# One stage for the seam between two layers of a graph network: gates, gated sum, second norm, layer-1 node products and the placing of logits in five groups of tiles

## The reference, cut to what matters

```python
xn = _layernorm(x)
x = x + gnn0(xn) + mix0(xn)
x = x + ffn0(_layernorm(x))            # four experts, mixed by gates
xn = _layernorm(x)                     # the "second norm"
x = x + gnn1(xn) + mix1(xn)            # mix1 ends in _layernorm(..) * ln2_g + ln2_b
x = x + ffn1(_layernorm(x))

# ffn0, end: a small graph attention gives 16 gate logits a node; normed, averaged over 4 heads
topk_s, topk_i = top_k(scores, 2); w = softmax(topk_s)
out = sum over experts ei of (where(topk_i == ei, w, 0).sum(-1)) * expert_ei(x)

# gnn1
Wh = (x @ W_w + W_b).reshape(N, 2, 128)
s = einsum('nhd,d->nh', Wh, a[:128]);  t = einsum('nhd,d->nh', Wh, a[128:])
e = leaky_relu(s[src] + t[dst], 0.2);  alpha = softmax of e over the edges of one src
agg = segment_sum(alpha * Wh[dst], src)
h = where(deg > 0, agg, Wh)            # a node without edges keeps its own Wh

# mix1: linear attention; keys first, over all nodes, then per chunk of nodes
kv = einsum(phi(k), v); out = phi(q) @ kv / (phi(q) . k_sum) @ Wo; two layer norms and a feed-forward
```

## Time and profile before

| | us |
|---|---|
| median of 3 runs | 4131.28 |
| lowest and highest run | 4127.74, 4132.18 |
| the profiled execution's own time | 4143.73 |
| its span | 4142.0 |
| PE busy in the span | 2283.8 (55%) |
| DVE busy | 1804.1 (44%) |
| ACT busy | 1391.3 (34%) |
| POOL busy | 1360.9 (33%) |

### The profile page before, as it was taken

The page is one execution under the profiler, slowest core; times in us unless marked ns, Lnnn a source line. Parts: engine busy times, 40 slices in busy tenths (PEclk is TensorE's granted clock), DMA queues, the critical chain, the costliest instruction groups (busy, mean ns, idle before and its releaser), DMA issues. The chain is left out here.

```text
span 4142.0 us, 47007 instructions
## 1 busy us (share of the span) xinstructions
PE 2283.8 (55%) x15074; PEld 1722.8 (42%) x15074; DVE 1804.1 (44%) x3989; ACT 1391.3 (34%) x3199; POOL 1360.9 (33%) x1327
## 2 busy tenths in 40 slices
PE   3777735441110113997563137435353663999998
PEld 3632425430110002655441125324342452679997
DVE  8898569820000000124899664424342547301112
ACT  2589256510000000122375011435353540223442
POOL 0000320047777773000000316544444413444442
PEclk9999867755555556997797568667676775899999
DMA  2300240021101110111231123433333321234544
GB/s 65 117 21 0 63 94 1 1 64 21 13 8 12 12 12 15 31 36 61 83 96 54 50 41 85 155 111 124 123 133 114 134 93 54 92 94 172 184 160 107
DMA packets 174189, 300.78 MB, mean 73 GB/s; under 512 B 82070, under 2 KB 133129, under 8 KB 163572
## 3 DMA queue, kind: packets, MB, share of 16 engines
q1 hardware_dynamic: 103592, 167.52, 13.4%
q0 software_dynamic: 70464, 131.75, 11.6%
HBM read 265.96 MB, written 105.32 MB: 90 GB/s over the span
## 5 line engine op out<-in xcount | busy, mean ns | idle before, releaser
L1794 POOL DMA_INDIRECT ge_near<-gat_src,s_other x512 | 518.8, 1013 | 169.7 <-issue 169.7
L2116 PE MATMUL bank<-arena 128*125 128x256 f32 x800 | 218.8, 437 | 630.0 <-issue 585.1
L2981 POOL DMA_INDIRECT he_buf<-wh_dram,s_other x400 | 386.3, 966 | 407.3 <-DVEq L3215 286.1
L2148 DVE TENSOR_TENSOR XN<-bank,arena 125x256 f32<-125x256 f32 (+1 forms) x100 | 42.4, 424 | 954.4 <-DMA g_al<-al_dram,g_idx 711.9
L2116 PEld LDWEIGHTS bank<-arena 128*125 128x125 f32 x800 | 170.2, 218 | 685.6 <-issue 626.0
L2129 ACT ACTIVATE arena<-bank,arena 128x500 f32<-128x500 f32 (+1 forms) x112 | 70.0, 633 | 933.5 <-DMA s_a_dram<-XN 486.1
L2661 ACT ACTIVATE x_hT<-bank,x_w 128x128 f32<-128x128 f32 x448 | 164.7, 368 | 262.4 <-PE bank L2604 227.7
L3101 ACT ACTIVATE he_buf<-he_buf,he_e 128x128 f32<-128x128 f32 x800 | 239.6, 387 | 37.3 <-issue 34.9
L1531 POOL IOTA gj_node<- 128x125 f32 x1 | 0.2, 242 | 673.8 <-POOLq L73 673.8
L2604 PEld LDWEIGHTS bank<-x_xT,x_w 128*128 128x128 f32 x1792 | 208.7, 192 | 2.8
L2604 PE MATMUL bank<-x_xT,x_w 128*128 128x128 f32 x1792 | 209.0, 275 | 0.0
(11 more groups left out here) (721 smaller groups left out, 5883.8 us busy)
## 6 DMA issues: line engine op xcount, KB each, us to landing
he_result<-he_buf SPq DMA_DIRECT2D x25, 2080.0 KB
XN<-s_a_dram SPq DMA_DIRECT2D x57, 512.0 KB
x_y<-XN SPq DMA_DIRECT2D x24, 448.0 KB
ge_near<-gat_src,s_other POOLq DMA_INDIRECT x512
x_x<-zero SPq DMA_DIRECT2D x1, 7196.0 KB, 38.1
x_xs<-x_x SPq DMA_DIRECT2D x56, 128.5 KB, 2.1
he_buf<-wh_dram,s_other POOLq DMA_INDIRECT x400
arena<-x_y SPq DMA_DIRECT2D x2, 2800.0 KB
```

The costliest lines, as they stand in the source:

```text
L1794: pool.indirect_dma_start(out=G[:, c, 0:HF + H], out_offset=None, in_=m.gat_src, in_offset=bass.IndirectOffsetOnAxis(ap=ed.other[:, c:c + ...
L2116: last = pe.matmul(m.ps[4 + j % 2][:P, 0:D], self.hT[:, f, j * P:(j + 1) * P], w.w2[e][:, f, :], start=f == 0, stop=f == FC - 1)
L2981: pool.indirect_dma_start(out=buf[j][:, c, 0:HF + H], out_offset=None, in_=m.wh_dram, in_offset=bass.IndirectOffsetOnAxis(ap=ed.other[:, t ...
```

## The change

Stages 2, 3 and 4 become one, `between_layers`, with one block, and the 25 scatters of stage 5 move into it. The 25 tiles are worked in five groups of 6, 6, 6, 5 and 2.

- The gates are computed as before (class `Gates0`).
- For the groups from the second on (`FIRST = 1`) POOL computes `y1 *= gate` and `X += y1`, two operations over a whole group. DVE adds the other three experts, and all four for the first group.
- After the sum of a group DVE takes its statistics and moments. ACT takes the square root, normalises the group's tiles (activation Identity with scale and bias), copies the transposes, and copies each product's row and logits out of PSUM.
- PE transposes the tiles of a group, then multiplies them. The bias enters as a third product with one row of ones.
- DVE adds the rows of a group to `X` two groups later, with no bias addition and no copy.
- POOL adds the shift of a group and scatters its logits to `hs_placed` tile by tile. `hs_placed` is now cleared by a DMA at the start of the stage, from a tile of zeros.
- SP issues all loads at the start of the stage, beside the gates, and stores rows and logits once a group, in two transfers each, split by partitions.
- In stage 5 POOL no longer clears `he_ke` nor scatters; it still waits for DVE's indices, since its own gather needs them. SP loads `he_ke` back right after the bounds.

```diff
@@ SpreadLogits
+    def reload(self, sp):
+        self.back(sp, self.raw, self.placed.rearrange("(p t) h -> p t h", p=128))
+    def first_own(self, pool):
         pool.wait_ge(self.idx_ready, 1)
         pool.indirect_dma_start(out=self.own[:, :], out_offset=None, in_=self.table,
                                 in_offset=bass.IndirectOffsetOnAxis(ap=self.first_i[:, :], axis=0)
                                 ).then_inc(self.own_sem, 16)
...
-def combine0(m, ex):
-            for e in (1, 2, 3, 0):
-                for t in range(NT):
-                    x = m.X[:, t * D:(t + 1) * D]
-                    dve.scalar_tensor_tensor(x, ex.place[e][:, t * D:(t + 1) * D], m.gate0[:, t, e:e + 1], x,
-                                             ALU.mult, ALU.add)
...
-class Gnn1Nodes(NodeProduct):
+class NodesBetween:
+    GROUPS = ((0, 6), (6, 12), (12, 18), (18, 23), (23, 25))
+    FIRST = 1
...
+    def sync(self, sp):
...
+        for lo, hi in self.GROUPS:
+            sp.wait_ge(self.kept, hi + 4)
+            self.stored.nodes(sp, near[:, lo:hi, 0:D], rows[:, lo:hi, :])
+            self.stored.nodes(sp, near[:, lo:hi, D:], self.logits[:, lo:hi, 0:H])
+        self.stored(sp, own, self.logits[:, :, H:])
         sp.wait_ge(self.stored.sem, self.stored.all)
...
+    def gpsimd(self, pool):
+        self.gates.gpsimd(pool)
+        pool.wait_ge(self.ex.back, 32 * self.ex.E)
+        pool.wait_ge(self.gates.ready, 1)
+        for lo, hi in self.GROUPS[self.FIRST:]:
+            x, y = (v[:, lo * D:hi * D].rearrange("p (t d) -> p t d", d=D) for v in (self.m.X, self.ex.place[1]))
+            pool.tensor_tensor(y, y, self.gates.gate[:, lo:hi, 1:2].broadcast_to((P, hi - lo, D)), ALU.mult)
+            pool.drain()
+            pool.tensor_tensor(x, x, y, ALU.add).then_inc(self.begun, 1)
...
+        for lo, hi in self.GROUPS:
+            pool.wait_ge(self.normed, hi)
+            x = self.m.X[:, lo * D:hi * D].rearrange("p (t d) -> p t d", d=D)
+            pool.tensor_tensor(x, x, self.shift[:, :].unsqueeze(1).broadcast_to((P, hi - lo, D)), ALU.add
                                ).then_inc(self.shifted, 1)
+            for t in range(lo, hi):
+                pool.wait_ge(self.kept, t + 5)
+                pool.indirect_dma_start(out=self.m.hs_placed,
+                                        out_offset=bass.IndirectOffsetOnAxis(ap=self.dst_i[:, t:t + 1], axis=0),
+                                        in_=self.logits[:, t, H:], in_offset=None,
+                                        bounds_check=128 * self.ed.cols - 1, oob_is_err=False).then_inc(self.placed, 16)
+        pool.wait_ge(self.placed, 16 * NT)
...
+    def vector(self, dve):
...
+        gates.vector(dve)
+        dve.wait_ge(self.ex.back, 32 * self.ex.E)
+        last = len(self.GROUPS) - 1
+        for g in range(last + 1):
+            combine(g)
+            if g:
+                norm(g - 1)
+            variance(g)
+            if g == 0:
+                self.prepare(dve)
+                self.places(dve)
+            if g >= 2:
+                add_rows(g - 2)
+        norm(last)
+        add_rows(last - 1)
+        add_rows(last)
+
+    def scalar(self, act):
...
+        for g, (lo, hi) in enumerate(self.GROUPS):
+            act.wait_ge(self.var_ready, g + 1)
+            act.sqrt(self.var[:, lo:hi], self.var[:, lo:hi]).then_inc(self.std_ready, 1)
+            act.wait_ge(self.norm_ready, g + 1)
+            for t in range(lo, hi):
+                act.activation(m.XN[:, t * D:(t + 1) * D], self.x(t), ACT.Identity, bias=self.less[:, t:t + 1],
+                               scale=self.rstd[:, t:t + 1]).then_inc(self.normed, 1)
+            for t in range(lo, hi):
+                act.wait_ge(self.turned, t + 1)
+                act.copy(xt[:, :, t * P:(t + 1) * P],
+                         m.ps[t % 4][:, 0:K2 * P].rearrange("p (k n) -> p k n", k=K2)).then_inc(self.moved, 1)
+            for t in range(lo, hi):
+                act.wait_ge(self.made, t + 1)
+                act.copy(self.row(t), m.ps[4 + t % 4][:P, 0:D])
+                act.copy(self.logits[:, t, :], m.ps[4 + t % 4][:P, D:self.ROW]).then_inc(self.kept, 1)
+
+    def tensor(self, pe):
...
+            for t in range(lo, hi):
+                pe.wait_ge(self.moved, t + 5)
+                pe.wait_ge(self.kept, t + 1)
+                bank = m.ps[4 + t % 4][:P, 0:ROW]
+                pe.matmul(bank, m.ones[0:1, 0:P], self.bias[0:1, :], start=True, stop=False)
+                for k in range(K2):
+                    last = pe.matmul(bank, m.XT[:, t * P + k * N:t * P + k * N + P], self.w[:, k, :],
+                                     start=False, stop=k == K2 - 1)
+                last.then_inc(self.made, 1)
...
@@ sums_and_mix1
-                edges.clear(pool)
                 x.mask(pool)
                 gather(0)
-                edges.gpsimd(pool)
+                edges.first_own(pool)
                 for t in range(1, nb):
                     gather(t)
...
                 x.load_keys(sp)
                 edges.bounds(sp)
+                edges.reload(sp)
                 x.load(sp)
-                edges.sync(sp)
```

More of the change, by code:

```diff
@@ L1969, in top_two @@
         done.then_inc(ready, 1)
-def gates0(m):
-    nc, io = m.nc, m.io
+class Gates0:
     H, E, C = 4, 4, 16
[L1976 to L2003, removed]
-                for t in range(NT):
[L2005 to L2042, removed]
@@ L2666, in scalar, with __init__ @@
             hidden(c)
-class Gnn1Nodes(NodeProduct):
+class NodesBetween:
     H, F = 2, 128
-    def __init__(self, m, s_logits, start):
-        super().__init__(m, "h1", D + 2 * self.H)
-        self.starts = start
+    GROUPS = ((0, 6), (6, 12), (12, 18), (18, 23), (23, 25))
+    FIRST = 1
+    def __init__(self, m, ex, ed):
+        self.m, self.ex, self.ed, self.ROW = m, ex, ed, D + 2 * self.H
+        self.gates = Gates0(m)
         m.wh_dram = m.dram("wh_dram", [N, D + self.H])
         m.s_dram = m.dram("s_dram", [N, self.H])
[L2680 to L2690, removed]
-        self.shifted = m.sem("h1_shifted")
-        self.bound_loads = Loads(m, "h1_bounds_loaded")
-    def load(self, sp):
-        io, F = self.m.io, self.F
@@ new lines, in __init__ @@
+        self.bound = place("h1_bound", [P, 2, NT])
+        self.none, self.dst = (place("h1_" + x, [P, NT]) for x in ("none", "dst"))
+        self.dst_i = place("h1_dst_i", [P, NT], I32)
+        self.st = place("h1_st", [P, NT, 6])
+        self.mean, self.var, self.tmp, self.rstd, self.less = (
+            place("h1_" + x, [P, NT]) for x in ("mean", "var", "tmp", "rstd", "less"))
+        self.rows = ex.place[1]
+        self.loads, self.shift_loads, self.bound_loads, self.cleared, self.stored = (
+            Loads(m, "h1_" + x) for x in ("loaded", "shift_loaded", "bounds_loaded", "cleared", "stored"))
@@ L2696, in load, with row @@
+    def row(self, t):
+        return self.rows[:, t * D:(t + 1) * D]
+    def sync(self, sp):
+        m, io, F, H = self.m, self.m.io, self.F, self.H
+        zeros = m.zero16[:, :].bitcast(FP32)[:, 0:self.ed.cols * H // 4]
+        with m.nc.allow_non_contiguous_dma(reason="one word per node"):
+            for i in range(2):
+                self.bound_loads(sp, self.bound_i[:, i, :], nodes_of(self.ed.start, i))
         self.loads(sp, self.w[:, :, 0:D], io["L1_gnn_W_w"].rearrange("(k p) d -> p k d", p=128))
@@ new lines, in sync @@
+        self.shift_loads(sp, self.shift[:, :], io["L1_mix_ln2_b"].partition_broadcast(P))
+        rows = self.rows.rearrange("p (t d) -> p t d", d=D)
+        near, own = (x.rearrange("(t p) c -> p t c", p=P) for x in (m.wh_dram, m.s_dram))
+        for lo, hi in self.GROUPS:
[3 more added lines that the diff above has]
+        self.stored(sp, own, self.logits[:, :, H:])
@@ L2742, in prepare, with places @@
         dve.drain().then_inc(self.w_ready, 1)
[L2744 to L2750 removed]
+    def places(self, dve):
         dve.wait_ge(self.bound_loads.sem, 32)
```

214 lines of the change are left out of this document (162 added, 52 removed).

## The result

The changed kernel takes 4167.81 us (median of 4 runs, 4163.45 to 4173.8) against 4131.73 for the kernel before: ratio 1.0094, 95% interval 1.0077 to 1.0111. It is 36 us slower, where 4132 had been forecast with a range up to 4154. The profiled execution took 4170.63 us, its span is 4168.9.

A forecast was written before the change was run, and what follows sets the result against it. A mostly serial DVE chain, then PE, bounds the seam; the loop whose sum frees POOL paces the stage behind. Terms of -5.9 and +6.7 us sum to +0.8, 4132 us on the median, range 4091 to 4154.

The forecast's parts named there:

- Gates, work on DVE: New stage, DVE's own work: gates 14.1 us, 81 gated sums of 0.401, statistics 8.3 and the rest, 80.4 in all.
- POOL's products in series with DVE's sums: New stage: POOL's 37.2 us add to DVE's chain instead of overlapping, giving 117.6; group 0's variance comes at 49.9.
- I take 127, since DVE and not PE sets the pace in every group: New stage: last tile's rows at 127 us, PE priced a quarter above full-clock time, DVE setting the pace.
- rival D: New stage: pauses between groups keep PE at half clock, rows end at 150, +17 us, kernel 4155; chance 0.14.
- The tail: End of new stage: last group's stores add 2.5 us; next stage begins 12.65 us after the last logit store.
- The slow condition moved onto the keys: Layer-1 stage, starting at S: gathers slow the keys, which end at S+131; first loop sum at S+167.5, +6.7 us.
- The rounds after it keep their shape, so the offset stays to the end.: Layer-1 loop: rounds after the first are unchanged, so the first loop sum's +6.7 us lasts to the end.
- The sum: Whole kernel: new stage -5.9 us plus layer-1 stage +6.7 us gives +0.8 us, 4132 us on the median.
- The first term: New stage: the next stage starts at 142.5 us instead of 148.4, -5.9 us.

## Why the prediction was wrong

- *Gates, work on DVE.* Right: 14.1 us for the gates, 0.41 a sum, 2.06 for six statistics.
- *POOL's products in series with DVE's sums.* Right: the first group's variance stood at 45 us after the start where 49.9 was forecast; without them the seam is 15.1 us shorter.
- *"I take 127, since DVE and not PE sets the pace in every group".* This step failed, and it is the miss. PE was priced at a quarter above its full-clock time; it ran at half clock throughout, which the prediction itself had named as the sign of rival D. The last logit store was issued 163.6 us after the start, not at 129.8. Full rows in the bias product give 39.1 of the 173.8 us back; the stage then takes 134.7 us, less than the 142.5 of the forecast, so the clock accounts for the whole miss of this term.
- *Rival D* had the right place (PE at half clock, each group behind it) and the wrong reason and size: it blamed pauses, and its 150 us let DVE and ACT work ahead. In fact ACT's square root for the next group stands behind its last copy, so normalising (3.06 us), transposes and six tiles of 3.18 us follow each other, 24.7 us a group.
- *The tail* was over-priced: 10.2 us from the logit store to the next stage, instead of 12.65.
- *The slow condition moved onto the keys.* Right: keys ended at S+134.7 (forecast S+131), the first loop sum came at S+171.9 (S+167.5), +10.3 us against +6.7. That it is this condition is shown twice: with the gathers held back the keys are on time, and where gathers slow nobody they are on time beside them. Its onset was read too narrowly, as 8 to 13 us into a run of gathers: ACT's weighting still took 0.30 us each until 2661.58, 16.6 us after the run's first gather at 2644.96.
- *"The rounds after it keep their shape, so the offset stays to the end."* Not borne out in the two profiled executions, where 8.7 of the 35.7 us were won back in the loop; one profile of each can't tell a gain from scatter.
- *The sum.* Forecast -5.9 + 6.7, measured +25.4 + 10.3. The first term is 31.3 us off, the second 3.6.

The rows chosen for the clock had full-row products only, 0.94 at 87% busy. The kernel before has one-row products in its loop, but they would not have warned of this: there the pair takes 0.69 us beside 0.70 for its full-row neighbour, at a clock of 1.00. Only a run with the one-row product in this very stream could have shown it. That PE would reach the full clock here was an assumption, not a reading.

## What to carry to other kernels

Before adding a bias by a one-row product in a stream where PE may become the bound, look at the clock with it in that stream; here padding it to full rows gave 39.1 us back, and the kernel before, which added it while copying out of PSUM, ran its products at 0.94. Don't give POOL a share of elementwise work while DVE's instructions have two SBUF inputs: here it cost 15.1 us. Work taken off a queue starts what stood behind it: look at what those transfers will run beside, and measure on more than one chip before a loop is arranged around a stall.

## What the runs showed of the hardware that was not expected

- With a one-row product in every tile PE stays at 1.2 GHz though it is busy 98% of 88 us (0.50); in the changed kernel's groups full rows brought it to 2.4 GHz within each group. The one-row pair is no shorter than the full-row pair at half clock (1.22 against 1.07 us). In the loop, among other products, one-row products ran at 2.4 GHz.
- The same kernel takes 4131 to 4151 us on some chips and 3193 to 3197 us on others. On the first, a long run of gathers on POOL slows the other engines: PE gets through one instruction in 1.56 us on average, ACT's weighting comes at 1.40 us each, and DVE's sums too, with nothing named that they wait for (first three lines, kernel before). On the others this is absent. The same 300 us of the first layer's experts, with POOL equally busy, hold 96 matmuls of PE in the kernel before on the first kind and 1164 in the changed kernel on the second (the two windows, in this order); of these 64 and 587 are on the line below, idle 228.1 and 17.3 us.

```profile
2604.99 0.49 DVE L3213 SCALAR_TENSOR_TENSOR he_buf<-he_buf,he_cont 128x256 f32<-128x256 f32 x1 [0.91 <-issue]
2606.40 0.48 DVE L3213 SCALAR_TENSOR_TENSOR he_buf<-he_buf,he_cont 128x256 f32<-128x256 f32 x1 [0.92 <-remote]
2607.79 0.49 DVE L3213 SCALAR_TENSOR_TENSOR he_buf<-he_buf,he_cont 128x256 f32<-128x256 f32 x1 [0.91 <-issue]
...
1000.00:1300.00 300.00, 40.95 (x96) 25.27 (x96) 3.40 (x8) 9.74 (x13) 224.57 (x229) 0.56 0.11 12
1000.00:1300.00 300.00, 261.07 (x1164) 174.07 (x1162) 77.86 (x174) 61.16 (x96) 226.25 (x232) 0.95 0.25 56
...
L2123 PE MATMUL bank<-arena 128*125 128x256 f32 x587 | 133.8, 386 | 17.3 <-ACT arena L2136 17.3
```

- On the first kind of chip, a pause of about 2 us after every eighth gather takes the condition away from the layer-1 stage and gives 232 us. What differs between the chips, and why a pause helps, these runs do not show. Each chip was used once, so they do not even show that the chip, and not the time of the run, makes the difference.
